# Layer 2 of a tile moved behind later dots, and late gathers tied to the dots, in a recommendation tower kernel

## The reference

```python
e = jnp.stack([tbl_0[ids[:, 0]], ..., tbl_25[ids[:, 25]]], axis=1)      # 512 x 26 x 128
sd = einsum('bfd,bd->bf', e, dense)                                     # 26 dots with the dense vector
ss = einsum('bfd,bgd->bfg', e, e); pairs = ss[:, iu, ju]                # the 325 pairs above the diagonal
h = concatenate([dense, sd, pairs, dense], axis=1)
h = maximum(h @ W_top1 + b_top1, 0.0)                                   # 512 wide
h = maximum(h @ W_top2 + b_top2, 0.0)                                   # 256 wide
y = h @ W_top3
```

## Time and profile before

| | |
|---|---|
| median of three runs | 116.11 us (114.59 to 116.14) |
| profiled execution, span from first to last instruction | 131.6 us |
| TensorE busy in it | 109.4 us, 83% |
| VectorE, ScalarE, GpSimd busy | 80.8, 65.6, 64.3 us |
| mean granted TensorE clock | 0.935 |

### The profile page before, as it was taken

How to read it: one execution, slowest core, us unless ns; L and a number is a source line. 1 busy time by engine, 2 the same in 40 slices (tenths; PEclk the granted TensorE clock), 3 DMA queues, 4 the chain that set the end, 5 groups by cost and what they waited for, 6 DMA issues and landing times.

```text
span 131.6 us, 2789 instructions
## 1 busy us (share of the span) xinstructions
PE 109.4 (83%) x1086; PEld 95.1 (72%) x1086; DVE 80.8 (61%) x218; ACT 65.6 (50%) x150; POOL 64.3 (49%) x66
## 2 busy tenths in 40 slices
PE   6999999199999998857798257990699997999794
PEld 6767888078868887947797146980669995999691
DVE  5799998798897999903088030385310886088101
ACT  4676560892975598503089300360730894087411
POOL 8477875675886778757167735276520000000000
PEclk9999999959999999996899977998569999999999
DMA  3987985359989812121102201021110000000000
GB/s 116 255 232 178 246 255 134 111 164 278 299 225 284 270 50 59 40 60 32 35 22 60 59 26 42 22 62 40 40 40 5 0 0 0 5 5 0 0 0 1
DMA packets 5030, 12.35 MB, mean 94 GB/s; under 512 B 1725, under 2 KB 1853, under 8 KB 5018
## 3 DMA queue, kind: packets, MB, share of 16 engines
q1 hardware_dynamic: 2906, 8.15, 21.2%
q0 software_dynamic: 1920, 3.94, 11.6%
q10 hardware_dynamic: 192, 0.10, 0.3%
HBM read 12.18 MB, written 0.00 MB: 93 GB/s over the span
## 4 chain that ended last, share of the span: by engine, by line
PE 65%; DVE 12%; issue 11%; ACT 6%; another core or an unknown queue 4%
PE dots L465 28%; PE dots L512 15%; DVE pairs L361 9%; PE hidden L537 4%; ACT pairs L299 4%; PE turned L492 4%; PE last_layers L441 2%; PE last_layers L554 2%; PE hidden L554 2%; PE dots L435 2%; PE last_layers L561 2%; PE turned L537 2%; PE last_layers L474 1%; DVE onehot L368 1%
## 5 line engine op out<-in xcount | busy, mean ns | idle before, releaser
L260 POOL DMA_INDIRECT rows<-tbl,gather_idx x60 | 61.6, 1027 | 31.7 <-issue 15.2
L361 DVE COPY pairs<-dots 27x128 f32<-27x128 f32 (+8 forms) x88 | 23.8, 270 | 21.1 <-PE dots L512 18.5
L299 ACT COPY pairs<-dots 27x128 f32<-27x128 f32 (+8 forms) x88 | 21.0, 238 | 29.0 <-PE dots L512 27.0
L368 DVE TENSOR_SCALAR onehot<-ids_h 125x512 fp32r<-125x512 f16 x88 | 33.0, 431 | 2.9 <-PE dots L465 2.0
L465 PE MATMUL dots<-onehot,high 125*128 125x512 f32 (+1 forms) x88 | 33.7, 401 | 0.0
L465 PE MATMUL dots<-onehot,low 125*128 125x512 f32 (+1 forms) x88 | 31.8, 380 | 0.1
L512 PE MATMUL dots<-embT 128*64 128x54 f32 x512 | 20.1, 241 | 8.5 <-issue 7.8
L512 PEld LDWEIGHTS dots<-embT 128*64 128x64 f32 x512 | 18.8, 155 | 10.4 <-issue 10.2
L313 ACT CAST high<-table 125x1024 fp32r<-125x1024 f32 (+1 forms) x12 | 11.7, 979 | 15.9 <-PE dots L465 12.6
L465 PEld LDWEIGHTS dots<-onehot,low 125*128 125x128 f32 x88 | 16.8, 193 | 3.7 <-DVE low L376 0.7
L465 PEld LDWEIGHTS dots<-onehot,high 125*128 125x128 f32 x88 | 17.0, 193 | 3.2
(11 more groups left out here) (46 smaller groups left out, 78.3 us busy)
## 6 DMA issues: line engine op xcount, KB each, us to landing
table<-tbl SPq DMA_DIRECT2D x10, 448.0 KB
wp<-w_pairs SPq DMA_DIRECT2D x2, 512.0 KB
rows<-tbl,gather_idx POOLq DMA_INDIRECT x60
table<-tbl SPq DMA_DIRECT2D x10, 52.0 KB
wd<-w_dense SPq DMA_DIRECT2D x1, 512.0 KB
w2s<-w SPq DMA_DIRECT2D x1, 512.0 KB
table<-tbl SPq DMA_DIRECT2D x2, 224.0 KB
denseT<-dense_t SPq DMA_DIRECT2D x1, 256.0 KB
```

Of the source, the lines that this page charges most:

```text
L260: pool.indirect_dma_start(out=rows[:, t % 2, n, :], out_offset=None, in_=tables[GATHERED_TABLES[n]][:, :], in_offset=bass.IndirectOffsetOn ...
L299: return nc.scalar.copy(dst, src)
L361: return nc.vector.tensor_copy(dst, src)
L368: nc.vector.tensor_scalar(onehot[:, i % 2, c, :], ids_h[:, i, :], float(c), None, ALU.is_equal).then_inc(onehot_ready, 1)
```

## The change

A token of layer 2 used to cover TensorE's matmuls and both relus; now M is the matmuls alone, H the two relus; likewise Y is layer 3's matmuls and V the copy of the result. The table of steps puts M0 behind D2 (before: ahead of it) and M1 at the end of the steps ahead of D3; R0 comes after C1.1 and R1 after C2.1 and B3.2. GpSimd holds gather 40 until one tile's dots are done, 46 until two, 53 until three, and nothing else; before, it held 40 and 51 on dots, 46, 48 and 53 on batches, and 55 and 57 on layer 1. Batch B3.3 is transposed in bank 0 of `dots`, waits there for tile 2's copies instead of for the placement of B3.2, and B3.2 is placed by ScalarE instead of VectorE.

```diff
-    HELD_BY_DOTS, HELD_BY_BATCH, HELD_BY_LAYER1 = {40: 1, 51: 2}, {46: 10, 48: 11, 53: 12}, {55: 1, 57: 2}
+    HELD_BY_DOTS = {40: 1, 46: 2, 53: 3}
...
-            D1 C1.0 B2.3 L0.0 L0.1 R0 C1.1 B3.0 M0 Y0
-            D2 C2.0 B3.1 L1.0 L1.1 R1 C2.1 P2 B3.2 M1 B3.3 Y1
-            D3 C3.0 L2.0 L2.1 R2 C3.1 P3 M2
-            L3.0 Y2 L3.1 R3 M3 Y3""".split()]
-
-        PLACERS = [0, 0, 0, 0, 0, 0, 0, 0, 1, 0, 1, 0, 1, 0, 1, 1]
+            D1 C1.0 B2.3 L0.0 L0.1 C1.1 B3.0 R0
+            D2 C2.0 B3.1 M0 L1.0 L1.1 C2.1 B3.2 R1 H0 Y0 V0 B3.3 M1 P2 H1
+            D3 C3.0 Y1 V1 L2.0 L2.1 R2 C3.1 P3 M2 H2
+            L3.0 Y2 V2 L3.1 R3 M3 H3 Y3 V3""".split()]
+
+        PLACERS = [0, 0, 0, 0, 0, 0, 0, 0, 1, 0, 1, 0, 1, 0, 0, 1]
...
+        LAST_BATCH = TILES * BATCHES - 1
...
-                    if k in HELD_BY_BATCH:
-                        pool.wait_ge(transposed, HELD_BY_BATCH[k])
-                    if k in HELD_BY_LAYER1:
-                        pool.wait_ge(layer1_done, HELD_BY_LAYER1[k])
...
         def transposes_of(n):
-            return last_layers[:, :].rearrange("p (a b) -> p a b", a=BATCH_T) if n == APART else turned
+            bank = {APART: last_layers[:, :], LAST_BATCH: banks[0]}.get(n)
+            return turned if bank is None else bank.rearrange("p (a b) -> p a b", a=BATCH_T)
...
                     if n == APART:
                         pe.wait_ge(table_placed, N_ONEHOT + 1)
+                    elif n == LAST_BATCH:
+                        for engine in range(2):
+                            pe.wait_ge(pairs_copied[engine], ALL * t)
```

More of the change, by code:

```diff
@@ L176, in dlrm_tower @@
         NAMES = {"T": "table", "D": "dots", "C": "copies", "B": "batch", "P": "dense", "L": "layer1", "R": "relu1",
-                 "M": "layer2", "Y": "layer3", "W": "warming"}
+                 "M": "layer2", "H": "relu2", "Y": "layer3", "V": "result", "W": "warming"}
         STEPS = [(NAMES[w[0]], *map(int, w[1:].split("."))) for w in """
@@ L339, in step @@
                                              ).then_inc(h1_ready, 1)
-                elif kind == "layer2":
+                elif kind == "relu2":
                     act.wait_ge(layer2_done, CHUNKS2 * t + 1)
@@ L405, in step @@
                                             ALU.add, ALU.max).then_inc(h2_ready[1], 1)
-                elif kind == "layer3":
+                elif kind == "result":
                     dve.wait_ge(layer3_done, t + 1)
```

## The result

The changed kernel took **119.06 us** (median of 121.37, 119.39, 118.72, 117.35), the kernel before 115.35 in the same comparison: a ratio of 1.039 with a 95% interval of 1.030 to 1.048. The medians of all runs give 1.032. Every ratio in this text leaves out runs more than 1.5% above the fastest of their kernel. The profiled one is the slowest of them, 121.37 us with a span of 119.4.

The account below looks back on a forecast made before the run. TensorE was taken to bound the kernel, with 65% of the chain of waits. Without halts, -1.85 + 3.85 + 0.5 = +2.5 us on 116.11 gave 118.6, plus 1.2 for the clock 119.8 us; range 113.4 to 121.4.

Parts of the forecast that it names:

- Tile 1's dots to tile 2's: From tile 1's dots' end, tile 2's wait for copies alone, starting at 6.75 us in place of 8.6: -1.85 us.
- Tile 2's dots to tile 3's: Added work and gather 59 ahead of tile 3's dots start them at 13.15 us in place of 9.29: +3.85 us.
- The two chains end within 0.3 us of each other: Behind tile 2's dots, ScalarE's chain through Y0 ends at 9.6 us, gather 59 lands at 9.9, the later.
- Behind tile 3's dots: Y1 stands ahead of layer 1, whose relu R2 stands ahead of ScalarE's last copies: +0.5 us.
- the clock: TensorE's new gap behind tile 2's dots halves the granted clock once: +1.2 us; none taken behind tile 1's dots.
- 12 to 14: Sign of being right: tile 3's dots start 12 to 14 us behind tile 2's, waiting for a gather.
- The base: First trace of the kernel before, 131.6 us, less 17.0 of halts gives 114.6; differences reckoned against the 116.11 median.
- halts: TensorE stopping, or its finished work reported late, around dots of tiles 0 and 1: 17.0 us, taken as nearly absent untraced.
- The rival of real halts: Halts stand in timed runs too, and clearing gathers 48 to 50 from tile 1's dots wins: 112.9 us, chance 0.17.
- 12.7 s: Most the change wins back around tile 1's dots if a share s of halts is real: s x (7.31 + 5.35).

Follow-up runs that it names:

- experiment 4: Changed kernel with TensorE's idle gaps filled by matmuls on zeros, against the kernel before: median 119.65 us, ratio 1.023.
- two by two: Tile 0's dots to end, full clock: kernel before 56.7 us, late holds alone 59.5; with gaps filled, new order alone 59.05, both 59.9.
- experiment 1: Kernel before, unchanged, traced a second time: 115.44 us with a span of 113.6; median of its four runs 116.75.
- experiment 6: Changed kernel, unchanged, run again against the kernel before: median 122.02 us, ratio 1.048.
- Experiment 7: Changed kernel with P2 ahead of Y0 instead of behind M1, against the kernel before: 138.97 us, ratio 1.015; second time, without halts, 1.029.
- experiment 8: Kernel before with only B3.3 in bank 0 of the dots and B3.2 placed by ScalarE: 138.39 us, ratio 1.008.
- experiment 9: Kernel before with only tile 0's layer 3 and its copy moved behind tile 2's dots: 138.24 us beside 138.28; again, 116.46 beside 115.98.
- experiment 5: Changed kernel with gaps filled and gathers held as in the kernel before: 141.79 us, ratio 1.033; again, median 119.38 beside 115.31.

## Why the prediction was right

**Forecast and sign.** The forecast was 119.8 us, slower by the wait and the bare work ahead of tile 3's dots; 119.06 was measured. Sign and mechanism were right. That the number came so close is in part luck: from tile 0's dots on the traces differ by 7.0 us (56.7 and 63.6), the medians by 3.7.

**Tile 1's dots to tile 2's: -1.85 forecast, -1.62 measured** (12.44 to 10.82). The copies set it. B3.0's gather was hidden with 0.8 us to spare in place of 1.2, since TensorE could start on it 5.4 us behind the dots, not 4.9.

**Tile 2's dots to tile 3's: +3.85 forecast, +4.3 measured at full clock** (13.25 to 17.54, experiment 4). The missing 0.4 is the landing: B3.3 starts 10.3 us behind the dots, I had 9.9. I had taken a gather as landed when its traffic is over. In the changed kernel gather 59 starts at 90.55; the traffic of 90.5 to 93.0, in 40 slices, is gathers 58 and 59:

```profile
GB/s 0 0 0 0 0 0 0 393 262 197 131 66 0 0 0 0 0 0 0 0 0 0 0 0 0 0 0 328 328 262 131 0 0 0 0 0 0 0 0 0
```

It is over at 92.4, and TensorE is released only at 93.07, 2.5 us behind the gather's start and not 2.1. "The two chains end within 0.3 us of each other" was 0.7 in the end (9.1 + 0.5 for Y0's end against 10.3), with the gather the later, as forecast. The two by two bears out what follows from it: taking away the late gathers alone gives back 0.9 us at full clock, the old order alone 0.4. One wait the prediction had at nothing: B3.1 waited 0.61 us for its gather in experiment 4, and layer 1 ended 6.6 us behind the dots in place of 5.95. That cost little, since B3.2's own gather starts 4.0 us behind the dots and so lands at 6.5.

**Behind tile 3's dots: +0.5 forecast, +0.55 measured** (20.24 to 20.79).

**The term that was mis-sized is the clock.** I took 1.2 us for one fall and none between tile 1's and tile 2's dots. In the profiled run both gaps led to a fall, and tile 3's dots started 15.8 us behind tile 2's, outside the "12 to 14" that was given as a sign of being right; at full clock it was 13.6. Stretches of the changed kernel, columns as before:

```profile
71.00:77.53 6.53, 4.36 (x44) 3.96 (x43) 5.88 (x22) 6.00 (x23) 5.01 (x6) 1.00 0.20 52
77.53:80.94 3.41, 3.41 (x73) 3.41 (x70) 0.61 (x1) 0.20 (x1) 1.30 (x2) 0.52 0.15 42
...
91.18:98.01 6.83, 5.96 (x27) 5.29 (x28) 1.43 (x3) 1.02 (x4) 0.32 (x1) 0.51 0.05 13
```

Behind two gaps of 1.3 and 0.8 us with B3.0 between them, tile 2's dots began at half clock (5.49 us in place of 3.94); the kernel before has one gap of 1.3 us there (experiment 1) and kept the full clock. The second fall lasted twice as long as the row I had priced it by. Together the falls cost 3.7 to 4.0 us (63.6 and 63.9 against 59.9), where I had 1.2. The timed runs hold them in part: of the four, one has a mean clock of 1.0 and a span of 115.5 us, the profiled one 0.957 and 119.4; in experiment 6, the two long runs aside, spans go from 116.7 at 0.985 to 121.2 at 0.944. Which fall a run without a trace had is not recorded.

**The base.** That 17.0 us had to be taken off the first trace before anything was added was right: 114.6 was reckoned, 113.6 measured as span. But not all of the 17.0 were halts: of the 2.08 us in tile 0's dots, 1.4 were matmuls at a lower clock (5.34 us busy in place of 3.96, clock 0.72). And the reason that I gave was not shown to be right. I took halts as absent from timed runs because the median was lower than the span. But in one session of experiments the *timed* runs of the kernel before took 138.28 us (17 runs, 136.18 to 139.85), and all four traces of that session, of changed forms of the kernel, are full of halts. Halts belong to a kind of execution, and the first trace and the first times came from different kinds. That session was also the only one on its chip, so the kind may as well be the chip's; no run here tells the two apart. Recording a profile doesn't bring halts by itself, for nine traces have none. Whether it has a part in them stays open: the listed timed runs have a span and a clock of their own, so there is no run here that is sure to be unrecorded.

**The rival of real halts** thus existed, but not in the comparison. Did the change help there? It was not run in that session. Experiment 7's kernel, which differs in P2 alone, was, and didn't gain: 1.015, medians 138.97 and 138.28 us. Tile 1's dots and tile 2's dots in its trace:

```profile
75.48:80.66 5.18, 4.02 (x126) 3.95 (x126) 1.08 (x1) 1.07 (x1) 0.00 (x0) 1.00 0.07 16
87.56:96.70 9.14, 7.02 (x129) 6.57 (x129) 1.07 (x1) 0.66 (x2) 1.52 (x2) 0.63 0.08 23
```

Tile 1's dots (the window leaves out their first 0.7 us) have 1.5 us of halts left; tile 2's, 3.96 us in the earlier trace rows, now take 9.14, of which 2.1 are halts beside gathers 51 and 52 and 3.1 the clock. By stages, stage 2 took 12.78 us beside 27.14 in experiment 8's trace of the same session, and stage 3 26.32 beside 13.38. What was won ahead of tile 2's dots came back behind them: the halts moved with the gathers, so "12.7 s" of that rival was too much even where halts are real.

## What to carry to other kernels

When a step moves out of one wait, follow it to the place where it lands: here 1.6 us won ahead of one tile's dots came back as 4.3 ahead of the next, as bare TensorE work behind a wait that another engine ended. The late gathers and a long chain on ScalarE ended together, so each undone alone gives back little. A gather has landed for TensorE when TensorE is released, not when its traffic is over: take the time from a row that shows the wait. And where a change opens new gaps on TensorE, even ones like the 1.3 and 0.8 us here, price the clock behind each of them, or put the work that has no hurry (here P2) into the gap.

## What the runs showed of the hardware

- The same program ran at 115 to 116 us in most sessions and at 138.28 in one, with TensorE stopping 0.2 to 1.2 us at a time inside dots. In these traces it does so beside gathers, while dots with none in flight run through (tile 3's in experiment 9's first trace, 4.09 us; tile 2's there, 3.94, with only the landing of the last one). The end of tile 0's dots in that trace:

```profile
61.92 0.21 PE L514 MATMUL dots<-embT 128*64 128x54 f32 x1 [0.40 <-issue]
62.63 0.34 PE L514 MATMUL dots<-embT 128*64 128x54 f32 x4 [0.51 <-issue]
64.05 4.23 PE L514 MATMUL dots<-embT 128*64 128x54 f32 x88 [1.08 <-issue]
```

  The groups of matmuls start 0.71 us or twice that apart; in the earlier trace rows it is the same 0.71. Yet gathers beside dots don't halt TensorE in the other sessions (tile 1's dots in experiment 1: 3.94 us with gathers running), so a gather alone is not enough. What else it takes is not shown.
- Matmuls on zeros kept the granted clock at 1.0 through both gaps (experiment 4, and experiment 5 with the gathers held as before).
- A gather of 128 rows takes GpSimd 0.94 us, and TensorE is released 2.5 us behind its start, some 0.6 us after its traffic is over (gather 59 in the changed kernel).
